# Moving a kernel's on-chip tiles so that those TensorE reads start at multiples of 512 bytes

## What is computed

```python
xn = layernorm(x)
gate, xBC, dt = split(xn @ in_proj_w.T)            # 8192, 10240, 128 columns
x, B, C = split(silu(causal_conv4(xBC)))
y = chunked_selective_scan(x, B, C, D, softplus(dt + dt_bias))   # chunks of 128 tokens
yg = y * silu(gate)
s = (group_rmsnorm(yg) * norm_w) @ out_proj_w.T
g = silu((silu(xn @ W1.T) * (xn @ W3.T)) @ W2.T)   # W1, W2, W3 unpacked from 4 bits
out = x + s * g
```

## Time and profile before

| | us |
|---|---|
| median of 3 runs | 1791.61 (1790.51 to 1792.0) |
| the profiled execution, first to last instruction | 1789.9 |
| TensorE busy | 1775.3 (99%) |
| weight loads busy (beside the matmuls) | 1462.1 (82%) |
| DVE, POOL, ACT busy | 1427.3, 1262.4, 1228.8 |

### The profile page before, as it was taken

The page is one execution under the profiler, slowest core; times in us unless marked ns, Lnnn a source line. Parts: engine busy times, 40 slices in busy tenths (PEclk is TensorE's granted clock), DMA queues, the critical chain, the costliest instruction groups (busy, mean ns, idle before and its releaser), DMA issues.

```text
span 1789.9 us, 30329 instructions
## 1 busy us (share of the span) xinstructions
PE 1775.3 (99%) x10357; PEld 1462.1 (82%) x10357; DVE 1427.3 (80%) x2196; ACT 1228.8 (69%) x2456; POOL 1262.4 (71%) x877
## 2 busy tenths in 40 slices
PE   8999999999999999999999999999999999999999
PEld 7788888888888888888888888888888888888877
DVE  7978878878788788788787887887887888878941
ACT  6986777777776777677866777677777677643320
POOL 5677787777777687677776786777776777676630
PEclk9999999999999999999999999999999999999999
DMA  5433333233333242333333342333333333235522
GB/s 200 160 123 101 99 130 107 93 121 107 117 107 110 96 134 94 102 110 116 119 104 95 118 122 96 115 98 117 115 96 111 107 123 101 77 108 162 151 78 94
DMA packets 122595, 202.84 MB, mean 113 GB/s; under 512 B 23056, under 2 KB 60560, under 8 KB 122192
## 3 DMA queue, kind: packets, MB, share of 16 engines
q1 hardware_dynamic: 120720, 197.32, 34.9%
q10 hardware_dynamic: 1728, 3.65, 0.5%
HBM read 193.57 MB, written 7.34 MB: 112 GB/s over the span
## 4 chain that ended last, share of the span: by engine, by line
PE 95%; DVE 3%; POOL 1%; issue 1%; DMA 1%; SPq 0%; ACT 0%; POOLq 0%; DVEq 0%; ACTq 0%
PE bank L137 16%; PE bank L135 16%; PE bank L136 16%; PE bank L543 11%; PE bank L585 7%; PE bank L631 7%; PE bank L633 6%; PE bank L632 6%; PE bank L831 3%; PE bank L693 3%; PE bank L674 1%; DVE z L1189 0%; PE bank L654 0%; DMA q_s<-w1s_dram 0%; DVE x_in L1341 0%
## 5 line engine op out<-in xcount | busy, mean ns | idle before, releaser
L1518 POOL TENSOR_TENSOR yt<-yt,ec 128x384 f32<-128x384 f32 x128 | 174.8, 1366 | 329.7 <-DVE ec L1253 329.7
L1189 DVE SCALAR_TENSOR_TENSOR z<-bank,cw_all,z 128x511 f32<-128x511 f32 (+2 forms) x477 | 356.3, 747 | 11.7 <-ACT z L944 0.5
L905 ACT ACTIVATE lm<-lm,hp 128x128 f32<-128x128 f32 x1024 | 313.2, 390 | 0.8
L1244 DVE TENSOR_TENSOR xdt<-bank,hp 128x512 f32<-128x512 f32 x128 | 88.3, 690 | 222.3 <-PE bank L693 221.0
L135 PE MATMUL bank<-xn_hi,conv_hi 128*128 128x512 f32 x640 | 261.7, 409 | 3.5 <-DVE z L1189 3.4
L1223 DVE SCALAR_TENSOR_TENSOR lm<-lm,gm 128x1024 f32<-128x1024 f32 x128 | 261.2, 2040 | 3.4 <-ACT lm L905 3.4
L137 PE MATMUL bank<-xn_hi,conv_lo 128*128 128x512 f32 x640 | 251.7, 393 | 0.0
L136 PE MATMUL bank<-xn_lo,conv_hi 128*128 128x512 f32 x640 | 250.5, 391 | 0.0
L1522 POOL TENSOR_TENSOR yt<-yt,gate 128x512 f32<-128x512 f32 x128 | 226.7, 1771 | 19.0 <-POOL yt L1518 0.9
L1527 POOL TENSOR_TENSOR conv_lo<-raw_x,conv_hi 128x512 fp32r<-128x512 f32 x124 | 218.4, 1762 | 9.9 <-ACT conv_hi L844 9.8
L944 ACT ACTIVATE z<-bank,cw_all 128x512 f32<-128x512 f32 x128 | 99.1, 774 | 166.5 <-PE bank L137 166.5
(11 more groups left out here) (145 smaller groups left out, 3950.9 us busy)
## 6 DMA issues: line engine op xcount, KB each, us to landing
lm<-cs_d SPq DMA_DIRECT2D x128, 512.0 KB, 4.0
raw_x<-w_conv_dram SPq DMA_DIRECT2D x128, 256.0 KB, 3.1
ec<-e_d SPq DMA_DIRECT2D x256, 96.0 KB, 3.6
raw_o<-w_out_dram SPq DMA_DIRECT2D x64, 256.0 KB, 2.7
raw_g<-w_gate_dram SPq DMA_DIRECT2D x61, 256.0 KB, 2.7
raw_b<-w_conv_dram SPq DMA_DIRECT2D x32, 256.0 KB, 3.4
q_raw<-w1q_dram SPq DMA_DIRECT2D x10, 256.0 KB, 3.8
q_s<-w1s_dram SPq DMA_DIRECT2D x10, 256.0 KB, 4.1
```

Source lines behind the costliest of these rows:

```text
L905: e = act.activation(lm[m % 3][:, u, :], lm[m % 3][:, u, :], ACT.Exp, bias=hp[bd.seq][:, Q_CS, k1, u:u + 1])
L1189: dve.scalar_tensor_tensor(dst[:, d:SEQ], src[:, 0:SEQ - d], cw_all[:, bd.group, pos, 3 - d:4 - d], dst[:, d:SEQ], ALU.mult, ALU.add).then ...
```

## The change

Eight small tiles (of which TensorE reads only `one`) move from further down the list to its head, one unused tile of 160 bytes (`to_line`) follows them, and `ident` comes behind it. Nothing else is changed: no instruction, shape, order, wait or transfer.

```diff
+        sh = alloc(ctx, "sh", [2, SH], I32)
+        rstd = alloc(ctx, "rstd", [NC])
+        rstd_sum = alloc(ctx, "rstd_sum", [NC])
+        neg_half = alloc(ctx, "neg_half", [8])
+        one = alloc(ctx, "one", [1])
+        nw_all = alloc(ctx, "nw_all", [GROUPS, TILES])
+        dc_all = alloc(ctx, "dc_all", [GROUPS, TILES])
+        cw_all = alloc(ctx, "cw_all", [GROUPS, CONVS, 5])
+        alloc(ctx, "to_line", [40])
         ident = alloc(ctx, "ident", [P])
         mask = alloc(ctx, "mask", [P])
-        sh = alloc(ctx, "sh", [2, SH], I32)
         xn_hi = alloc(ctx, "xn_hi", [KT, SEQS * SEQ], R32)
         xn_lo = alloc(ctx, "xn_lo", [KT, SEQS * SEQ], R32)
...
         b_t = alloc(main, "b_t", [SEQ])
-        cw_all = alloc(main, "cw_all", [GROUPS, CONVS, 5])
         gate_hi = [alloc(main, f"gate_hi{h}", [KT, HALF], R32) for h in range(2)]
         gate_lo = [alloc(main, f"gate_lo{h}", [KT, HALF], R32) for h in range(2)]
         c_t = alloc(main, "c_t", [2, SEQ])
-        nw_all = alloc(main, "nw_all", [GROUPS, TILES])
-        dc_all = alloc(main, "dc_all", [GROUPS, TILES])
         xt = alloc(main, "xt", [4, SEQ])
...
         hp = [alloc(main, f"hp{h}", [NQ, TILES, 2 * NC]) for h in range(2)]
-        rstd = alloc(main, "rstd", [NC])
-        rstd_sum = alloc(main, "rstd_sum", [NC])
-        neg_half = alloc(main, "neg_half", [8])
-        one = alloc(main, "one", [1])
```

## The result

The changed kernel takes 1780.78 us (median of 4 runs, 1780.4 to 1781.06) against 1791.34 (4 runs, 1790.51 to 1792.0): 0.9941 of the time, 95% interval 0.9929 to 0.9953, 10.6 us faster. Forecast were 1779 us and 12.5 us.

A forecast was written before the change was run, and what follows sets the result against it. TensorE's matmul stream was taken to bound the kernel; savings of 6.4 + 4.9 + 1.2 = 12.5 us gave 1791.6 - 12.5 = 1779.1 us, predicted as 1779, with a range of 1764 to 1794 us.

The forecast's parts named there:

- The bound: Whole kernel: TensorE busy 99% of the span, so matmul time shows one for one; other engines have a fifth in hand.
- The pattern: Split matmuls: equal remainders to 512 settle at 0.2267 us, 64 apart stays 0.2335; following something unlike disturbs six to eight matmuls.
- Item 1: 128 gate tiles: operand difference goes from 64 to 0, conv tile's pace of 2.29 for 2.34 us, 6.4 us saved.
- Item 2: 122 output tiles behind gate tiles: disturbed start goes if gate settles and remainders agree, 2.72 for 2.76 us, 4.9 us saved.
- Item 3: 30 B and C projections behind output tiles: settled 2.49 for 2.53 us, 1.2 us saved.
- Items 4 to 6: Conv tiles (bounds 0 and 2.9 us), plain float32 matmuls, and everything else including other engines and transfers: 0 taken for each.
- Nothing happens: Gate tiles' slow pace comes from PSUM bank or neighbours, which the change leaves: 1790 to 1794 us, chance 0.18.
- The remainder itself costs: Split matmuls pay 0.0133 us each, perhaps for starting off a multiple of 512 bytes: 1735 or 1696 us, chance 0.13.
- Slower: Equal remainders hurt plain float32 matmuls at lines 543 and 585: 1799.5 us, or 1813 if both pay; chance 0.07.

The follow-up runs named there:

- run 1: Changed kernel with the 160-byte pad made 320, so every tile starts at remainder 160 to 512: 1780.87 us, 0.9943 of the kernel before.
- run 3: Changed kernel without to_line: xn, conv and output operands at remainder 352, gate tiles (with c_t, b_tok, lm) at 416: 1789.71 us, 0.9993 of before.
- 4 for the other families: Four kernels without to_line, conv, gate and up operands apart by 256, 64, 32 or 128 bytes, output and down by others: 1783.3, 1801.3, 1807.8, 1802.4 us.
- run 2: Kernel before with cw_all alone moved to the front (xn, conv, gate at remainder 224, output operands left at 352): 1780.75 us, 0.9941 of before.
- run 5: Changed kernel with xdt, xw and state alone 128 bytes further: 1776.56 us, 0.9921 of the kernel before.
- u160: Changed kernel with every tile at remainder 160 to 512 (pad of 320 bytes): 1780.87 us.
- d256: Kernel without to_line, stationary operands of conv, gate and up tiles 256 bytes further than xn, output 256 and down 352: 1783.3 us.
- xdt128: Changed kernel with xdt, xw and state alone 128 bytes further: 1776.56 us.
- x64: Changed kernel with xdt, xw and state 64 bytes further: 1779.4 us, one run.
- x192: Changed kernel with xdt, xw and state 192 bytes further: 1779.06 us, one run.

## Why the prediction was right

**The bound.** Right. TensorE without idle time from 80 to 1600 us before and after, and what its streams lost (10.5 us) is what the span lost (10.8) but for waits.

**The pattern.** Its first half was right and is now shown: the difference counts and the shared remainder doesn't (runs 1 and 3, and 4 for the other families). It was read too coarsely in two ways: 256 counts as 0, and for 256 columns some differences make the pace faster. The sentence that anything from a region with another remainder disturbs the next tile was wrong as put: in run 2 the output tile steps by 128, loses 4 ns in its first distance and keeps 0.227. The projections for B and C were disturbed by a step from 352 to 160 and not by one from 352 to 224. The output tile of the kernel before had two things against it, a gate stream in front that never settled and a step of 192 in the moving operand, a size of step that disturbs the B and C tiles. Run 2 takes both away; run 3 takes away the step alone, and the tile stays disturbed, by the unsettled stream or by the step of 64 in the stationary operand.

**Item 1, gate tiles.** Forecast 6.4 us, measured 4.4. The term was mis-sized because I gave the gate tile the conv tile's start. Both do start disturbed behind plain matmuls, but the gate tile takes 10 matmuls to settle and the conv tile 6 (in ns, the ten distances sum to 2308 and 2292, 16 ns a tile or 2.0 us for 128). With the start of run 5 the gate tiles are 368.5 - 360.8 = 7.7 us better than before, so the term had the right bounds (0 and 9.6) and the wrong neighbour.

**Item 2, output tiles.** Forecast 4.9, measured 4.5. A settled gate tile in front does it in run 2, and an unsettled one undoes it in run 3; the equal remainder, the other half of that item's condition, was hardly needed for a step of 128: in run 2 output tiles sum to 350.0 us against 349.3.

**Item 3, projections.** Forecast 1.2, measured 1.3.

**Items 4 to 6.** Forecast 0, measured 0.3 for conv tiles and nothing for the rest.

**The sum.** 12.5 forecast, 10.5 measured, nearly all of the gap from item 1. The range of 1764 to 1794 us held the unchanged time as well, so that the result fell in it says little; the terms say more.

**The rivals.** "Nothing happens" is out; the up projection with a difference of 64 shows that neither bank nor neighbours made the gate tiles slow. The Trainium skill, "SBUF — State Buffer", section "Who interferes with whom", gives TensorE two independent read ports and has it never wait on anyone; here the measurements decide otherwise as to the independence, as the place of a load moves the pace of a stream from 0.2268 to 0.2333 us. "The remainder itself costs" is out by run 1 and by the unchanged 0.2268 of the up projection; the 0.0133 us that each matmul pays beyond its columns stayed at every equal remainder, fell to some 0.011 in the halves of 256 columns that lay 192, 224 or 352 apart, and has no explanation here. (The matmuls that this rival counts add up to 5,751, not 5,770, which changes nothing.) The 216 ns of the Trainium skill, "TensorE: Matmul & The Clock Gate", section "Back-to-back issue gap", are its gap for a single matmul of 512 columns, and for a stream of loads and matmuls it gives 131; the prediction took the first for a stream's pace. Neither was reached by any float32r stream here; the fastest settled one took 227. "Slower" is out: plain matmuls at equal remainders cost what they did, and run 5 gains by giving them unequal ones.

## What to carry to other kernels

Where float32r matmuls of 512 columns that each load new weights run back to back, write down the addresses of stationary and moving operand; if they differ by anything but a multiple of 256 bytes, try to make them agree, which here took the move of one 1600-byte tile. Judge it by the distance from start to start in a long even stream, and look at how many matmuls each tile needs until it settles, as that can change with the place of tiles that it doesn't read. For 256 columns measure first, since three unlike differences were 2% faster there. A small tile put in the middle of an allocation list can cost 0.6%, and in a bad case (32 bytes between the operands of most streams) 1.5% against the good layout.

## What was not expected of the hardware

- A float32r matmul of 128 by 128 by 512 that loads its own weights settles at 0.2267 us where load and stream lie 0 or 256 bytes apart (mod 512), and at 0.2294 to 0.2340 at each of the seven other differences tried. At 256 columns it takes 0.120 at 0 and 0.118 at 192, 224 and 352.
- Many disturbed streams walk the same path back: 229, 233, 236, 224, 231, 236, 228, 233, 231, 227 ns (to 1 ns) in the gate tiles of the changed kernel and of the variants u160, d256, xdt128, x64 and x192, and in the B and C projections of the kernel before; conv tiles enter that path at its fifth step (231, 236, 228, 232, 231, 227). The conv tiles of run 2 walk another.
- Where a tile enters depends among other things on the offsets of the plain float32 operands around it, though these matmuls themselves keep their pace at every difference tried (sums of 169.6 or 169.7 and 105.2 us in all 14 kernels).
